# A four-layer graph network on one core: gather in pairs of transfers, normalizations and rank weights on ACT, rank sums on PE

## The reference

```
layer 0: relu(D^-1/2 (A+I) D^-1/2 (h W0))
layer 1: [h, Gh, G^2 h, G^3 h] W^T + b        with G the scaled A+I
layer 2: drop some neighbours of nodes with more than 10; then per node and per
         feature sort the neighbours' values and take 0.25*q(0.25) + 0.5*q(0.5)
         + 0.25*q(0.75) of them (linear interpolation); a two-layer MLP of h + that
layer 3: A (h W3) + b
```

## Time and profile before

| | |
|---|---|
| median of 3 runs | 2798.1 us (2797.18 to 2803.76) |
| the profiled execution | 2827.46 us |
| its span, first to last instruction | 2825.7 us |
| mean granted TensorE clock | 0.701 of full speed |
| PE, weight loads, DVE, ACT, POOL busy | 1535.0, 858.3, 1625.1, 462.6, 1299.3 us |
| idle POOL time ahead of gathers, 16 times | 1087.0 us |
| idle DVE time before L1223 | 407.5 us under "remote", 12 times, and 135.9 us under PE and "issue" |
| idle ACT time before its copies of `ps_tr` L604 | 888.7 us |

### The profile page before, as it was taken

The page is one execution under the profiler, slowest core; times in us unless marked ns, Lnnn a source line. Parts: engine busy times, 40 slices in busy tenths (PEclk is TensorE's granted clock), DMA queues, the critical chain, the costliest instruction groups (busy, mean ns, idle before and its releaser), DMA issues.

```text
span 2825.7 us, 24253 instructions
## 1 busy us (share of the span) xinstructions
PE 1535.0 (54%) x8885; PEld 858.3 (30%) x8997; DVE 1625.1 (58%) x2443; ACT 462.6 (16%) x756; POOL 1299.3 (46%) x1196
## 2 busy tenths in 40 slices
PE   3735637556374655638366464836636375565232
PEld 2412414323142332314233241423314243233111
DVE  2511827649285574928467383755828376494926
ACT  3101212102021120202112020210302121020000
POOL 1072370735527173552717447172643707265550
PEclk9766658667586766759577676866768586777555
DMA  3122130313213131321313123131322313112120
GB/s 99 54 25 53 46 55 21 75 11 86 19 40 62 24 75 12 83 22 34 67 20 77 15 53 54 29 69 8 88 18 50 55 22 75 10 23 20 23 24 4
DMA packets 106610, 120.13 MB, mean 43 GB/s; under 512 B 71486, under 2 KB 71614, under 8 KB 106430
## 3 DMA queue, kind: packets, MB, share of 16 engines
q0 software_dynamic: 36864, 37.82, 14.2%
q1 hardware_dynamic: 69566, 79.98, 9.2%
HBM read 109.27 MB, written 8.45 MB: 42 GB/s over the span
## 4 chain that ended last, share of the span: by engine, by line
DVE 40%; PE 24%; issue 18%; another core or an unknown queue 15%; ACT 2%; DVEq 1%; POOL 0%; DMA 0%; POOLq 0%; ACTq 0%; SPq 0%
PE ps_tr L596 7%; DVE lists L1181 4%; DVE slots L1001 4%; PE ps_tr L604 4%; DVE slots L1000 3%; PE ps_prod L615 3%; PE ps_tr L585 2%; PE ps_misc L775 2%; DVE slots L1008 2%; DVE slots L1009 2%; DVE xc L977 1%; DVE stat L979 1%; DVE stat L976 1%; PE ps_misc L704 1%
## 5 line engine op out<-in xcount | busy, mean ns | idle before, releaser
L403 POOL DMA_INDIRECT slots<-h_rows,row_no x1152 | 1287.4, 1118 | 1433.2 <-DVEq L1187 1087.0
L596 PE MATMUL ps_tr<-adj_t,y_mid 128*128 128x512 bf16 x960 | 301.7, 459 | 223.7 <-issue 121.3
L1223 DVE TENSOR_TENSOR y_mid<-ps_prod,scales 128x512 f32<-128x512 f32 x48 | 33.2, 692 | 554.2 <-remote 407.5
L448 ACT ACTIVATE columns_t<-ps_tr 128x512 f32<-128x512 f32 (+1 forms) x192 | 113.0, 595 | 1409.2 <-PE ps_tr L604 888.7
L596 PEld LDWEIGHTS ps_tr<-adj_t,y_mid 128*128 128x128 bf16 x1024 | 105.6, 112 | 471.1 <-issue 416.0
L1181 DVE MAX8 lists<-ps_key 128x8 f16<-128x1024 f32 x128 | 157.8, 1233 | 112.8 <-PE ps_key L685 69.4
L585 PE MATMUL ps_tr<-h_t,w_l_sb 65*128 65x512 f32 x192 | 151.3, 896 | 107.6 <-issue 76.1
L695 PE MATMUL ps_misc<-parts_w,select_t 128*128 128x64 bf16 x384 | 36.7, 220 | 268.1 <-issue 229.3
L472 ACT ACTIVATE adj_n<-adj_f 128x1024 f16<-128x1024 f32 x128 | 134.3, 1050 | 229.1 <-remote 80.7
L604 PE MATMUL ps_tr<-adj_t,low 128*64 128x512 bf16 x1024 | 157.9, 419 | 16.9 <-issue 16.6
L615 PE MATMUL ps_prod<-both_ident,columns_t 128*128 128x64 f32 x768 | 107.9, 297 | 101.6 <-issue 91.6
(11 more groups left out here) (210 smaller groups left out, 2539.2 us busy)
## 6 DMA issues: line engine op xcount, KB each, us to landing
adj_f<-in_adj SPq DMA_DIRECT2D x128, 512.0 KB
slots<-h_rows,row_no POOLq DMA_INDIRECT x1152
x<-in_x SPq DMA_DIRECT2D x16, 256.0 KB
h_rows<-h SPq DMA_DIRECT2D x16, 256.0 KB, 2.9
out<-x SPq DMA_DIRECT2D x16, 256.0 KB
xc<-in_L_gnn_W SPq DMA_DIRECT2D x1, 64.0 KB
w_sb<-in_L_gnn_W SPq DMA_DIRECT2D x2, 32.0 KB
h_rows<-zeros SPq DMA_DIRECT2D x2, 32.0 KB, 1.5
```

The lines of the kernel that those rows point to most:

```text
L403: pool.indirect_dma_start(out=slots[:, slot_of(par, s), t * C:(t + 1) * C], out_offset=None, in_=table[par][:, :], in_offset=bass.Indirect ...
L448: act.activation(dst, view, ACT.Copy, scale=scale).then_inc(tr_free, 1)
L596: nc.tensor.matmul(dst[:, :], top_halves(pair_of)[:, j, :], adj_t[g % 3][:, columns[j]], start=(j == 0 and not begun), stop=False)
```

## The change

**The gather.** A group is now two transfers (`PAIR`), and the two semaphores alternate from pair to pair. Ahead of a pair POOL waits until the last pair but one has landed. The waits by tile are gone.

**The rank sums.** DVE no longer weighs and no longer adds. After `sort_6` it sets `sorted_ready`, and ACT multiplies each of the 7 narrow ranks in each of the 8 tiles by its weight in place: 56 ACTIVATEs of 128x64 (`weigh`). 13 more weigh the wide ranks (`weigh_wide`) after `merge_rest`. PE adds: `sum_wide` sums the 13 wide ranks by 13 matmuls with the identity; DVE splits that sum (`wide_parts`). `turned_sums` then takes the place of `spread_wide`, of `aggregate` and of the transposes of the sum: for each tile 1 matmul of the node's own row, 3 for the wide parts and 7 for the ranks add up, already turned, in PSUM. It stands between v2 and v3, where the transposes stood.

**The normalizations.** DVE keeps the sum over features (`norm_begin`), and the reciprocal and two small products (`norm_scale`). ACT squares with an accumulated sum, tile by tile (`norm_spread`, 8 ACTIVATEs), takes the root, and applies scale, shift and Relu tile by tile (`norm_apply`, 8 ACTIVATEs). `h1`, `h2`, `y` and `z` are so written by ACT. `y`'s split on DVE now comes after `row_numbers`.

**The order.** `mlp_rows` on PE moves ahead of the first `row_keys`, `add_mlp` on DVE ahead of the first `row_list`. ACT casts tiles 5 to 7 of the next adjacency after the weighing, not before v1's second half. Both `h3` copies stand at the end of ACT's turn.

```diff
@@ gather, POOL @@
-                def row(column, s, t, k):
+                def landed(k):
+                    at_least(pool, gathered[par][k], issued[k] * 16)
+
+                def row(column, s, t):
+                    k = sum(issued) // PAIR % 2
+                    if sum(issued) % PAIR == 0:
+                        landed(k)
                     issued[k] += 1
...
                 for t in range(T):
-                    k = t // BURST_TILES % 2
-                    if t % BURST_TILES == 0:
-                        landed(k)
                     for s in range(1, SLOTS):
-                        row(t * SLOTS + s - 1, s, t, k)
-                landed(0)
-                row(COLS * SLOTS, 0, WIDE_A, 0)
+                        row(t * SLOTS + s - 1, s, t)
+                row(COLS * SLOTS, 0, WIDE_A)
...
@@ ACT @@
+            def norm_spread(name, g):
+                _, less_mean, var, std, _, _ = stat_of(name)
+                act.wait_ge(mean_ready, NORM[name, g] + 1)
+                for t in range(T):
+                    last = act.activation(square[:, t * C:(t + 1) * C], x[g % 4][:, t * C:(t + 1) * C], ACT.Square,
+                                          bias=less_mean[:, t:t + 1], accum_out=var[:, t:t + 1])
+                last.then_inc(squared, 1)
+                act.wait_ge(squared, NORM[name, g] + 1)
+                act.activation(std, var, ACT.Sqrt, bias=eps_col[:, :], scale=1.0 / C).then_inc(std_ready, 1)
+
+            def norm_apply(name, g, to, ready):
...
+                    last = act.activation(to[:, t, :], x[g % 4][:, t * C:(t + 1) * C], ACT.Relu,
+                                          bias=shift[:, t:t + 1], scale=rstd[:, t:t + 1])
...
+            def weigh(g, first, last):
+                par = g % 2
+                act.wait_ge(sorted_ready, g + 1)
+                for t in range(first, last):
+                    for s, wire in RANKS:
+                        value = slots[:, slot_of(par, s), t * C:(t + 1) * C]
+                        wire = SLOTS - 1 - wire if par else wire
+                        done = act.activation(value, value, ACT.Copy, scale=weight[par][:, t, wire:wire + 1])
+                    done.then_inc(weighed, 1)
...
@@ PE @@
+            def turned_sums(g):
+                par = g % 2
                 pe.wait_ge(wide_summed, g + 1)
...
+                for i in range(2):
+                    tr_turn(f"agg.{i}", g)
+                    for t in range(i * (T // 2), (i + 1) * (T // 2)):
+                        pe.wait_ge(weighed, g * T + t + 1)
+                        dst = tr_bank(f"agg.{i}", g)[0:C, t % (T // 2) * P:(t % (T // 2) + 1) * P]
+                        nc.tensor.matmul(dst, h2[par][:, t * C:(t + 1) * C], ident_f[:, :], start=True, stop=False)
+                        for k in range(3):
+                            nc.tensor.matmul(dst, parts_w[:, k, :], select_t[g % 3][:, t * P:(t + 1) * P],
+                                             start=False, stop=False)
+                        for s, wire in RANKS:
+                            last = nc.tensor.matmul(dst, slots[:, slot_of(par, s), t * C:(t + 1) * C], ident_f[:, :],
+                                                    start=False, stop=(wire == SLOTS - 1))
+                    last.then_inc(tr_full, 1)
...
@@ DVE @@
+            def norm_begin(name, g):
+                total, less_mean, _, _, _, _ = stat_of(name)
+                step(v.tensor_reduce(total, tiles(x[g % 4]), AX.X, ALU.add))
+                step(v.tensor_scalar(less_mean, total, -1.0 / C, None, ALU.mult))
+                dve.sem_inc(mean_ready, 1)
...
-            def narrow_weighing(g):
-                weigh(g, 2, 3, 1, 2)
-                weigh(g, 10, 3, 2, 2)
-                weigh(g, 15, 1, 7, 1)
```

225 lines of the change are left out of this document (108 added, 117 removed).

## The result

Forecast: 2903 us, range 2130 to 2990. Measured: 3010.98 us, median of 4 runs (3008.03 to 3011.29), against 2800.93 for the kernel before: 1.074 times, 95% interval 1.069 to 1.078. The direction was right, the size half of what came (102 us of 210), and the range ended 21 us short. In the profiled execution (3011.29 us, span 3009.5) PE is busy longer and DVE shorter than in the earlier trace rows, as forecast.

A forecast was written before the change was run, and what follows sets the result against it. Bound: waits, with PE's signals late while POOL issues the gather at full pace. 14 turns at +7.5 us add 105 to the profiled 2827.46, giving 2932; less 29 for the median, 2903 us, range 2130 to 2990.

The forecast's parts named there:

- Step 1, the pairs: Gather on POOL: pauses of 1 to 3 us against 1.6 us of relief from DVE, net 0.
- The stall stays: PE's late signals until the gather ends: small pauses at pairs would not end DVE's 42 us wait; chance 0.50.
- I set one against the other: 0: Gather length: 1 to 3 us of added pauses and 1.6 us of relief taken to cancel.
- my 1.6 us: Gather beside DVE: some 3 us less of large DVE instructions would shorten it by 1.6 us.
- Steps 2 to 4: DVE's dropped work, PE's sums, last stretch: v3's product 18 us later, stretch 9 to 10 shorter; net +8 a turn.
- an absorbed wait of 1.4: Before v3's product: about 1.4 us of an old wait for `low` is absorbed, lowering the added cost to 18 us.
- The sum: Whole kernel: 14 turns at +7.5 us give +105; the two last turns, without b, add nothing worth a term.
- The pairs did not end the stall: Rival that the pairs do end it: turns of 124 us, some 2140 us in all, 2050 to 2350; chance 0.25.
- the point named for it: Gather on POOL: the pairs-end-the-stall rival decides from some 0.2 to 0.3 us of pause for each transfer.
- ACT is held as PE is: Rival: ACT's ACTIVATEs last to the gather's end, 6 to 10 us more a turn, 3020 us; chance 0.06.
- the root at 1219: ACT's root at 1219 passed unhindered; used as the argument against ACT being held.
- That profiling makes the stall: Instruction records could hold PE in the profile only; the median 1% under the profiled execution spoke against it.

The follow-up runs named there:

- norms_bursts: Changed kernel with narrow ranks weighed and summed on DVE again and the gather's waits of before, normalizations left on ACT: 2725.2 us (0.965).
- singles: Each transfer waits for the last but one (PAIR = 1), in both kernels: 2361.9 us (0.837) for the kernel before, 2350.7 (0.833) for the changed one.
- bursts: Gather waits as in the kernel before, by groups of whole tiles; put back into the changed kernel they gave 3045.8 us (1.078).
- before_two_one: Kernel before with the gather in groups of two and one transfers by turns, each group waiting for the last but one: 2211.1 us (0.790).
- after_two_one: Changed kernel with the gather in groups of two and one transfers by turns, each group waiting for the last but one: 2433.3 us (0.865).
- sets 1 to 4: Four of five sets of follow-up kernels, each on its own chip; the kernel before took 2826.6, 2803.9, 2824.9 and 2800.7 us beside them.
- two and one: Gather in groups of two and one transfers by turns, each group waiting for the last but one; in the kernel before 2211.1 us (0.790).

## Why the prediction was right and wrong

**The bound** was read rightly: the kernel is set by a stall that the gather's pace makes and its end ends. The runs with pauses (0.83, 0.79, and 0.84 with no landing to wait for) show it; at the end of gather 6 the changed kernel's POOL still issues each 1.25 us, as in the earlier trace rows, but for a pause at a pair:

```profile
1288.57 0.95 POOL L420 DMA_INDIRECT slots<-h_rows,row_no  x1 [0.30 <-issue]
1289.82 0.94 POOL L420 DMA_INDIRECT slots<-h_rows,row_no  x1 [0.31 <-issue]
1291.91 0.95 POOL L420 DMA_INDIRECT slots<-h_rows,row_no  x1 [1.14 <-DMA slots<-h_rows,row_no]
1293.16 0.95 POOL L420 DMA_INDIRECT slots<-h_rows,row_no  x1 [0.30 <-issue]
```

**Step 1, the pairs.** "The stall stays" held. Pauses were 3.3 us a gather by the list of waits, 2.3 without the 0.3 us that stands before any transfer, against 1 to 3:

```profile
POOL slots L420 <- DMA slots<-h_rows,row_no: 53.4, 54, 3.0
```

"I set one against the other: 0" holds for turns of the same kind: 167.0 with pairs in the kernel before, 166.9 without, and at most 2.1 us of gain in the changed kernel. What it missed is that pairs let some turns of the kernel before get a hand-off or two further while the gather runs, 6.4 us a turn in the mean; the changed kernel has no such turn. By the Trainium skill, "SBUF — State Buffer", section "Who interferes with whom", the one that issues second is blocked for the other's whole instruction; an estimate from that is that 3 us of such instructions less take 3 us off a gather, and the traces do not show it. Gathers 1 to 14 last 105.2 us in the mean and 102.9 before, and the difference is what the pauses add, so neither 3 nor my 1.6 us came off.

**Steps 2 to 4, a turn.** +7.5 forecast, +7.6 measured, and in turns of the same kind both parts are near their terms. With `mlp_rows` moved (3 us), the normalizations were to give -7; norms_bursts gives -6.4. The sums were to cost 15 (16.3 less an absorbed wait of 1.4); they cost 16.1. These lengths are from three chips, and 1 us is within what a chip makes, so that 7.5 and 7.6 are so close is in part luck. turned_sums itself took 18.0 where 17.3 was said, at 0.21 us for a rank's matmul in place of 0.25, and sum_wide 1.2 in place of 0. The stretch behind v3's product is 21.8, within 21 to 27. What no step had: the normalizations alone would have gained 10.7 in the mean, through short turns, and with the sums on PE there was none of these.

**The step that failed is "The sum", with its words "the two last turns, without b, get the sums on PE (17) for 13 of DVE: nothing worth a term"**, and that the last turn with b was counted as one of 14 alike. Three pieces make up the miss of 108 us: 54 in the tail, 26 in the last turn with b, 29 in the step from the profiled execution to the median. The tail: +54. Its bare part, 15 to 18 us (the lower figure is that of the kernels with singles), I had as 4: behind the last gather ACT's weighing has no stall to hide in. ACT in order of time, for c = 15:

```profile
2939.25 10.13 ACT L498 ACTIVATE slots<-slots,weight 128x64 f32<-128x64 f32 x42 [30.10 <-DVEq L1324]
...
2949.28 3.20 ACT L506 ACTIVATE merged<-merged,weight 128x64 f32<-128x64 f32 x13
2952.39 3.43 ACT L498 ACTIVATE slots<-slots,weight 128x64 f32<-128x64 f32 x14
```

PE begins the wide sum only behind the wide ranks' weighing, at 2952.5. The other 36 follow from my own reading, and I did not apply it: PE is held while POOL issues, DVE is not, and the sums of c = 14 lie beside gather 15. Second, the last turn with b: +33 for 7.5. Before, it was one of the short turns: DVE got v1's product at 2547.33 and v2's at 2559.75, while the gather ran, as it does in that turn of all three profiled kernels with bursts or pairs and the sums on DVE. That ACT has no casts in that turn may be why, but is not shown, and middle turns with casts can be short too. After, it is held at v1 and lasts as long as the middle turns. DVE in order of time in that turn, before and after:

```profile
2547.33 0.69 DVE L1223 TENSOR_TENSOR y_mid<-ps_prod,scales 128x512 f32<-128x512 f32 x1 [3.49 <-issue]
```

```profile
2694.56 0.69 DVE L1264 TENSOR_TENSOR y_mid<-ps_prod,scales 128x512 f32<-128x512 f32 x1 [56.82 <-remote]
```

Either the weighing ahead of v1's copies or PE's added hand-off may keep it in the stall until the gather's end; moving the first alone did not free it. Third, the 29 us: I took the median of before as 29 below its profiled execution and carried that over; after, the two are 0.3 apart.

**The rivals.** The pairs did not end the stall; the point named for it, 0.2 to 0.3 us of pause for each transfer, was a good guess: POOL's waits for landings in before_two_one are 358.2 us at 327 of 1152 transfers, 0.23 for each transfer without the usual 0.3 us, and DVE's longest wait for v1 or v2 under "remote" is 10.7 us there; but in after_two_one, with about as many (383.1), it does not suffice. "ACT is held as PE is" was right as a mechanism and wrong in its price. My argument against it, the root at 1219, did not bear on it, since PE was held only from 1220.9. In the changed kernel's last turn with b, ACT and PE in order of time:

```profile
2657.42 0.35 ACT L498 ACTIVATE slots<-slots,weight 128x64 f32<-128x64 f32 x1 [1.05 <-issue]
2658.82 0.35 ACT L498 ACTIVATE slots<-slots,weight 128x64 f32<-128x64 f32 x1 [1.05 <-issue]
...
2663.74 0.27 PE L747 MATMUL ps_misc<-merged,ident_f 128*128 128x64 f32 x1 [2.54 <-issue]
2666.55 0.27 PE L747 MATMUL ps_misc<-merged,ident_f 128*128 128x64 f32 x1 [2.54 <-issue]
```

ACT executes one ACTIVATE in 1.4 us, PE one matmul and its weight load in 2.8. But the weighing is nearly always done before that begins (in gather 6 from 1232.60 to 1250.0, at full rate): in the whole run it loses at most 8.8 us so, at 12 of 896 ACTIVATEs:

```profile
ACT slots L498 <- issue: 8.8, 12, 1.1
```

That profiling makes the stall is excluded: by the Trainium skill, "NOTIFIC — the notification-queue block", section "Overflow: three behaviours, one of which stalls the engine", records could hold an engine, but unprofiled runs take the same time, 3008.03 to 3011.19 against 3011.29.

Open: what in the chip holds PE back, why four chips do it (those of sets 1 to 4) and one does not, and the cause of the last turn with b beyond what is said. Open too is how many transfers it takes until PE is held: in gather 6 POOL issued at 1.25 us from 1238.1 on, and PE executed 26 matmuls at full rate at 1247.0 and was held from 1257.8. Late loading of instructions is not the cause there: from 1255 to 1305 the queues that bring instructions moved one packet of 16 KB, at 1303, when PE was at full rate again. And on none of the chips was ACT's share in the cost of the sums measured by itself.

## What to carry to other kernels

When one engine is slowed by another's traffic, price moved work by where it lies, beside the traffic or behind it: 18 us of sums were 18 after a gather and 53 beside one. Count the first and last turns of a pipeline apart; they have other covers, and here held 87 of 184 us. Look at each turn before you trust a mean: 6.4 and 10.7 us "a turn" were 0 and 6.4 in most turns and 11 to 26 in a few. And when a stall ends with some engine's burst of issues, pace the burst first: `PAIR = 1` gained 16%, two and one 21%, more than all the work moved between engines; but try it on several chips.

## What the runs showed of the hardware

POOL's gather transfers at 1.25 us without a pause slow PE, after some 20 us of them in gather 6, to 4 matmuls in 10 us; the signal of PE's wide sum, finished at 1252.7, reached DVE at 1299.9. ACT is held too (one ACTIVATE in 1.4 us); DVE is not (gather 2 of the kernel before). A transfer each 1.63 us with a memset between leaves PE free, and so does an average pause of 0.23 us if PE has no more than the kernel before's work. The effect depends on the chip: the kernel before takes 2801 to 2827 us on four, 2091 on a fifth, and pauses of two and one gain 21% on two of those, where a version with somewhat more pauses costs 3% on this. ACT's scaling of 128 x 64 fp32 takes 0.34 us alone and 0.24 from start to start in a row.
